# Cross-attention and a block-quantised feed-forward layer on one core: the first two steps in another order

## The reference

```
n   = layernorm(x)
k,v = split((ctx @ Wsrc.T + b_src) * mask)          # 8 heads of 16
q   = (n @ Wtgt.T + b_tgt) * mask
att = softmax(where(mask == 0, -inf, q k / 4)) v     # per sequence and head
x   = x + concat(n, att) @ Wout.T + b_out
g   = fp4(layernorm(x)) @ fp4(w_gate).T              # fp4: blocks of 16 along the last axis
u   = fp4(layernorm(x)) @ fp4(w_up).T
x   = x + fp4(silu(g) * u) @ fp4(w_down).T
```

## Time and profile before

| | |
|---|---|
| median of 3 runs | 218.21 us (218.11 to 219.34) |
| the profiled execution | 219.57 us |
| its span | 217.6 us |
| mean granted TensorE clock | 0.973 |
| loaded and stored | 11.97 MB |

### The profile page before, as it was taken

How to read it: one execution, slowest core, us unless ns; L and a number is a source line. 1 busy time by engine, 2 the same in 40 slices (tenths; PEclk the granted TensorE clock), 3 DMA queues, 4 the chain that set the end, 5 groups by cost and what they waited for, 6 DMA issues and landing times.

```text
span 217.6 us, 5689 instructions
## 1 busy us (share of the span) xinstructions
PE 187.8 (86%) x2045; PEld 141.5 (65%) x2045; DVE 176.5 (81%) x391; ACT 131.8 (61%) x264; POOL 139.3 (64%) x203
## 2 busy tenths in 40 slices
PE   0839988979998999998998998796898988899963
PEld 0318574856967769587696775475676766677753
DVE  6417785898799876978769987999999999999941
ACT  2362697957878877798786744364455383665441
POOL 6272737188969592672926577676689875777750
PEclk9985999999999999999999999699999999999998
DMA  6999632040200000000000000000101010101111
GB/s 190 268 293 345 225 115 81 7 144 3 96 3 5 3 0 0 5 3 3 0 3 5 0 5 0 0 0 2 50 3 48 0 48 3 48 2 51 48 49 48
DMA packets 13665, 11.97 MB, mean 55 GB/s; under 512 B 766, under 2 KB 10558, under 8 KB 13630
## 3 DMA queue, kind: packets, MB, share of 16 engines
q1 hardware_dynamic: 13078, 11.29, 16.8%
q10 hardware_dynamic: 560, 0.33, 0.5%
HBM read 9.52 MB, written 2.10 MB: 53 GB/s over the span
## 4 chain that ended last, share of the span: by engine, by line
PE 31%; POOL 20%; issue 14%; DVE 7%; ACT 4%; POOLq 0%; DVEq 0%; ACTq 0%
POOL hq L372 7%; POOL wq_y L357 5%; PE bank L890 4%; PE bank L946 4%; PE bank L949 3%; PE bank L899 3%; PE bank L900 2%; PE bank L878 2%; PE bank L970 2%; POOL xn L254 2%; ACT xn L411 2%; PE a_pair L841 2%; POOL sch L364 2%; PE bank L841 2%; ACT val L423 2%
## 5 line engine op out<-in xcount | busy, mean ns | idle before, releaser
L970 PE MATMUL bank<-wdT,hT 128*128 128x128 f32 x192 | 27.1, 278 | 4.1 <-issue 3.3
L946 PE MATMUL bank<-guT,xqT 128*128 128x352 f32 x64 | 25.5, 481 | 4.3 <-DVE hh L732 4.3
L372 POOL TENSOR_TENSOR hq<-wq_u,sch 128x704 f32<-128x704 f32 x16 | 22.6, 1410 | 9.5 <-DVE wq_u L759 9.4
L970 PEld LDWEIGHTS bank<-wdT,hT 128*128 128x128 f32 x192 | 23.9, 191 | 5.4 <-issue 4.4
L949 PE MATMUL bank<-guT,xqT 128*128 128x352 f32 x64 | 25.0, 473 | 0.0
L357 POOL TENSOR_TENSOR wq_y<-hh,ivh 128x704 f32<-128x704 f32 x16 | 22.5, 1407 | 3.9 <-DVE ivh L747 3.3
L878 PE MATMUL bank<-cT,wsT 128*128 128x512 f32 x32 | 16.9, 655 | 6.5 <-DMA cT<-in_ctxT 6.5
L477 ACT ACTIVATE mask_bc<-bank 128x352 f32<-128x352 f32 x32 | 14.7, 458 | 12.3 <-PE bank L946 12.3
L545 ACT COPY hT<-bank 128x384 f32<-128x384 f32 x32 | 15.2, 476 | 10.2 <-PE bank L958 10.2
L532 ACT ACTIVATE a_pair<-wq_y 128x704 f32<-128x704 f32 x16 | 12.2, 763 | 14.8 <-DVE wq_u L759 14.4
L612 DVE TENSOR_REDUCE den<-prob 128x8 f32<-128x512 f32 x32 | 19.8, 666 | 0.0
(11 more groups left out here) (117 smaller groups left out, 497.2 us busy)
## 6 DMA issues: line engine op xcount, KB each, us to landing
cT<-in_ctxT SPq DMA_DIRECT2D x8, 512.0 KB, 5.2
x_all<-in_x SPq DMA_DIRECT2D x8, 256.0 KB, 5.5
mask_bc<-in_mask_rows SPq DMA_DIRECT2D x8, 256.0 KB, 6.3
out_y<-mask_bc SPq DMA_DIRECT2D x8, 256.0 KB, 2.2
wsT<-in_WsT ACTq DMA_DIRECT2D x1, 256.0 KB, 4.2
w_all<-in_wg SPq DMA_DIRECT2D x1, 176.0 KB
w_all<-in_wu SPq DMA_DIRECT2D x1, 176.0 KB
w_all<-in_wd SPq DMA_DIRECT2D x1, 176.0 KB
```

Source lines behind the costliest of these rows:

```text
L372: nc.gpsimd.tensor_tensor(hq[i][:, :, 0:I].rearrange("p t (n k) -> p t n k", k=BLK), rh[i][:, :, :].rearrange("p (t n) k -> p t n k", t=2) ...
L946: nc.tensor.matmul(gu_bank[2 * n % 3][:, 0:I], xqT[g % 2][:, t], guT[:, 0, :], start=True, stop=True).then_inc(pe_g, 1)
L970: last = nc.tensor.matmul(d_bank[:, j * P:(j + 1) * P], hT[n % 2][:, c, :], wdT[:, c, :], start=(c == 0), stop=(c == 2))
```

## The change

The loads of the mask are cut in two: the columns of group 0 are loaded by themselves, two of four pieces on SP behind the first x and context, two on ScalarE's queue behind wsT; the rest follows on ScalarE's queue. The order on SP becomes x0, context 0, mask pieces, mask row 0, x1, context 1, the three weights, mask row 1, x2, and so on. POOL makes neg_mask of group 0 before the reciprocal deviation of group 0, and no bias nb for that group; VectorE normalises group 0 itself. On TensorE, 34 matmuls on constants run at the start; in step 0 only keys, transposes and queries of group 0 remain. Step 1 begins with the scores of group 0, then the values of group 0 and the keys of group 1; the bias of the values stands behind the values of group 1. VectorE's weight scales move from step 0 to step 1 ahead of the masked queries, the statistics of group 2 behind them, and the bias sum behind the reciprocals of the row sums. POOL's wq_y, the deviations of groups 2 and 3 and `add_bias(0)` move into step 1. From step 2 on ScalarE runs `normalise1` at the head of a step, ahead of `weight_evac` and `v_evac`.

```
# SP
             load_x(0)
             load_c(0)
+            sp.wait_ge(mb_zero, 1)
+            for p in range(PAIRS // 2):
+                load_pairs(sp, p, slice(0, TILES), ld_mb0)
+            load_m(0)
             load_x(1)
-            load_m(0)
-            sp.wait_ge(mb_zero, 1)
-            for p in range(PAIRS):
-                sp.dma_start(mask_b[32 * p:32 * p + 2, :, :]...).then_inc(ld_mb, 16)
+            load_c(1)
             sp.wait_ge(w_zero, 2)
             ...
-            load_c(1)
+            load_m(1)
             load_x(2)
...
# POOL
-            rstd1_of(0)
-            pool.wait_ge(ld_mb, 16 * PAIRS)
+            pool.wait_ge(ld_mb0, 16 * PAIRS)
             pool.wait_ge(mb_zero, 1)
             nc.gpsimd.tensor_scalar(neg_mask[:, tiles(0), :], ...).then_inc(nm_ok, 1)
+            rstd1_first()
             rstd1_of(1)
+            pool.wait_ge(ld_mb, 16 * PAIRS)
...
-            rstd1_of(2)
-            add_bias(0)
...
-                if on(g1) and g1 > 0:
-                    add_bias(g1)
-                if k == 0:
+                if k == 1:
                     pool.wait_ge(wiv_ok, 1)
                     nc.gpsimd.tensor_tensor(wq_y[:, :, :], ...).then_inc(wy_ok, 1)
+                    rstd1_of(2)
+                if on(g1) and g1 > 1:
+                    add_bias(g1)
...
                 if on(g2):
                     expand_reciprocals(g2)
-                if on(g1 + 3):
+                if k == 1:
+                    add_bias(0)
+                    add_bias(1)
+                    rstd1_of(3)
+                if on(g1 + 3) and k > 0:
                     rstd1_of(g1 + 3)
# ScalarE
             act.dma_start(wsT[:, :, :], ...).then_inc(ld_ws, 16)
+            act.wait_ge(mb_zero, 1)
+            for p in range(PAIRS // 2, PAIRS):
+                load_pairs(act, p, slice(0, TILES), ld_mb0)
...
-            normalise1(0)
+            act.wait_ge(mb_zero, 2)
+            for p in range(PAIRS):
+                load_pairs(act, p, slice(TILES, NT), ld_mb)
             def attn_step(k):
+                if on(g1) and k > 1:
+                    normalise1(g1)
                 if 0 <= k - 5 < 3:
                     weight_evac(k - 5)
                 if on(g2):
                     v_evac(g2)
...
-                if on(g1) and k > 1:
-                    normalise1(g1)
# VectorE
+            def normalise_first():
+                dve.wait_ge(rstd1, 1)
+                dve.wait_ge(aggr1, 1)
+                for j in range(TILES):
+                    last = nc.vector.tensor_scalar(xn[0][:, j, :], x_all[:, j, :], mv1[:, j, 0:1],
+                                                   rs1[:, j:j + 1], ALU.subtract, ALU.mult)
+                last.then_inc(xn_ok, 1)
...
+                if k == 1:
+                    weights_scales()
                 if on(g1):
                     q_masked(g1)
-                if k == 0:
-                    dve.wait_ge(bo_pe, 1)
-                    dve.wait_ge(ld_o, 32)
-                    (b_out sum)
-                    weights_scales()
+                if k == 1:
                     stats1(2)
                 (row sums, reciprocals)
                 if k == 1:
+                    (b_out sum, with its two waits)
                     stats1(3)
# TensorE
+            def warm_up():
+                for _ in range(34):
+                    nc.tensor.matmul(av_bank[:, 0:P], neg_ident[:, :], neg_ident[:, :], start=True, stop=True)
             pe.wait_ge(c_id, 3)
+            warm_up()
             def attn_step(k):
                 if on(g2):
                     scores(g2)
+                if k == 1:
+                    v_project(0, 0)
+                    v_project(0, 1)
+                    k_project(1)
...
                     q_project(0)
-                    bias_of_values()
                 elif on(g1):
                     xn_transpose(g1)
-                    k_project(g1)
+                    if k > 1:
+                        k_project(g1)
...
-                if on(g1):
+                if on(g1) and k > 0:
                     v_project(g1, 1)
+                if k == 1:
+                    bias_of_values()
```

More of the change, by code:

```diff
@@ L139, in xattn_ffn @@
         ld_m = [sem(f"ld_m{g}") for g in range(NG)]
-        ld_ws, ld_wt, ld_b, ld_o, ld_fw, ld_mb = (sem(n) for n in ("ld_ws", "ld_wt", "ld_b", "ld_o", "ld_fw", "ld_mb"))
+        ld_ws, ld_wt, ld_b, ld_o, ld_fw, ld_mb0, ld_mb = (
+            sem(n) for n in ("ld_ws", "ld_wt", "ld_b", "ld_o", "ld_fw", "ld_mb0", "ld_mb"))
         out_d = [sem(f"out_d{s}") for s in range(2)]
@@ L176, in past, with load_pairs @@
                 eng.wait_ge(semaphore, value)
+        def load_pairs(eng, p, t, loaded):
+            eng.dma_start(mask_b[32 * p:32 * p + 2, t, :].rearrange("b n s -> b (n s)"),
+                          mask_pairs[:, t.start * S:t.stop * S]).then_inc(loaded, 16)
         block = ctx.enter_context(nc.Block())
@@ L212, in _ @@
             sp.dma_start(b_out[:, 0, :], bo.to_broadcast([P, D])).then_inc(ld_o, 16)
-            load_m(1)
             load_x(3)
@@ L228, in _, with rstd1_first @@
         def _(pool):
+            def rstd1_first():
+                pool.wait_ge(aggr1, 1)
+                nc.gpsimd.tensor_scalar(ve1[:, tiles(0)], mv1[:, tiles(0), 1], EPS, 1.0, ALU.add, ALU.mult).then_inc(var1, 1)
+                pool.wait_ge(var1, 1)
+                nc.gpsimd.tensor_tensor(rs1[:, tiles(0)], ve1[:, tiles(0)], minus_half[:, :], ALU.pow).then_inc(rstd1, 1)
             def rstd1_of(g):
@@ L235, in rstd1_of @@
                 pool.wait_ge(rstd1, g + 1)
-                pool.wait_ge(nm1_ok, g + 1)
+                pool.wait_ge(nm1_ok, g)
                 nc.gpsimd.tensor_tensor(nb1[:, tiles(g)], nm1[:, tiles(g)], rs1[:, tiles(g)], ALU.mult).then_inc(nb1_ok, 1)
@@ L310, in _ @@
                                     ALU.mult, ALU.add).then_inc(nm_ok, 1)
+            rstd1_first()
             rstd1_of(1)
+            pool.wait_ge(ld_mb, 16 * PAIRS)
+            pool.wait_ge(mb_zero, 2)
             nc.gpsimd.tensor_scalar(neg_mask[:, TILES:, :], mask_b[:, TILES:, :], BIG, -BIG,
@@ L405, in normalise1 @@
             def normalise1(g):
-                act.wait_ge(nb1_ok, g + 1)
+                act.wait_ge(nb1_ok, g)
                 act.wait_ge(ld_x[g], 16)
@@ L567, in _ @@
         def _(dve):
-            nc.vector.memset(mask_b[:, :, :], 0.0).then_inc(mb_zero, 1)
+            nc.vector.memset(mask_b[:, 0:TILES, :], 0.0).then_inc(mb_zero, 1)
+            nc.vector.memset(mask_b[:, TILES:, :], 0.0).then_inc(mb_zero, 1)
             nc.vector.memset(w_all[64:P, 0:WBLK, :], 0.0).then_inc(w_zero, 1)
@@ L585, in stats1 @@
                 stats(g, st1, mv1, stat1, aggr1)
+            def normalise_first():
+                dve.wait_ge(rstd1, 1)
+                dve.wait_ge(aggr1, 1)
+                for j in range(TILES):
+                    last = nc.vector.tensor_scalar(xn[0][:, j, :], x_all[:, j, :], mv1[:, j, 0:1], rs1[:, j:j + 1],
+                                                   ALU.subtract, ALU.mult)
+                last.then_inc(xn_ok, 1)
             def stats2(g):
@@ L681, in _ @@
             nc.vector.tensor_scalar(bk_of[:, :], head_of[:, :], b_k, None, ALU.mult).then_inc(c_bk, 1)
+            normalise_first()
             stats1(1)
@@ L712, in attn_step @@
                 if k == 1:
+                    dve.wait_ge(bo_pe, 1)
+                    dve.wait_ge(ld_o, 32)
+                    nc.vector.tensor_tensor(b_out[:, 0, :], o_bank[:, 0:D], b_out[:, 0, :], ALU.add).then_inc(bo_ok, 1)
                     stats1(3)
```

2 lines of the change are left out of this document (removed).

## The result

The changed kernel takes 213.59 us (median of 4 runs, 212.46 to 216.25), the kernel before 218.5 us on the same chip. The ratio is 0.9743, with a 95% interval of 0.9689 to 0.9797: 2.6% faster. The forecast was 211.2, in a range of 208.8 to 214.8.

What follows compares the result with a forecast made beforehand. The prediction took the start as bound by order of work on TensorE, not a resource. 5.4 us head start at step 2 plus 1.6 in steps 5 to 7 gives 7.0; 218.2 - 7.0 = 211.2, range 208.8 to 214.8.

Steps and rivals of the forecast that it cites:

- main case: Whole kernel: the forecast with its unknown costs of mask rows, VectorE's normalise and step 1; 210 to 213 us, chance 0.57.
- the clock falling before 14: TensorE at the start: a granted clock falling before 14 us would show the prediction wrong.
- Mask rows at 6.6: Start: split mask pieces of group 0 land between 6.5 and 7.3 us, taken as 6.6, instead of 11.24.
- Rival (a): Start: mask rows land late, at 11.24; first scores slip 4.6 us, gain 2.4, time 215.8; chance 0.11.
- xn ready at 9.2: Group 0: normalised x ready at 9.2 us after neg_mask, variance, power and VectorE's normalise, against 10.0 before.
- First scores at 12.4: TensorE, group 0: scores start at 12.4 us after transposes, copy, queries and masked queries, instead of 19.78; 7.4 us earlier.
- Step 1 takes 12.8 us: Group 0 scores to group 1 scores: 10.84 becomes 12.8 us; scores -0.75, values 2.1, uncovered copy 0.4, bias 0.25.
- Rival (c): Steps 1 and 2: x or context of group 2 or 3 lands late, giving 214.2 to 216.6 us; chance 0.10.
- (d): VectorE in step 1 waits at the weight scales for late weights, making the kernel slower; chance 0.03.
- Rival (e): TensorE's 1.59 us stop in `attend(1)` moves where it waits anyway; gain 8.6, time 209.6; chance 0.12.
- Steps 5 to 7, 1.6 us: ScalarE's normalise ahead of value copies removes TensorE's 0.53 us stop before the transposes, three times: 1.6 us.
- rival (b): Start: warm-up fails to raise the clock or gaps let it fall; about 5 us more, time 216; chance 0.07.

Runs made afterwards that it cites:

- first profile: Traced execution of the changed kernel, compared with the kernel before: 216.25 us, span 214.5, the granted clock falling in the queries of group 0.
- second profile: Trace from timing the changed kernel again, nothing altered, beside the kernel before: span 211.3; that run's median 213.31 us, ratio 0.9737.
- the two edits filled: Kernel before with the bias sum moved and ScalarE's normalise first, plus 76 matmuls of 128 columns in TensorE's step 0 gaps: 215.39 us, ratio 0.9833.

## Why the prediction was right

The sign and the range were right; the median came out 2.4 us above the forecast. It lies above the 210 to 213 of the main case too, in the part of the range that was kept for late mask rows and late loads, and neither of these happened; what came in their place was a shorter head start, the base below and, in the longest execution, the clock. The ratio, taken on the 218.21 us that the prediction started from, gives 212.6, inside the main case. So the range is right either way, but the median is in it partly by luck. One of the signs of being wrong, the clock falling before 14, was there in the first profile (0.62 at 12.5 to 13.4), and with it a slow value block. By the steps of the prediction, against the second profile of the changed kernel, in which the clock holds:

- **Mask rows at 6.6.** Right, 6.51 (6.24 in the first profile). Rival (a) is out.
- **VectorE's normalise, 0.8.** 1.11, near the upper bound of 1.16.
- **xn ready at 9.2.** Wrong, 10.3. The step that failed is what is queued behind what: I listed the work behind `rstd1_first` on VectorE, but not `bk_of`, ahead of the normalise there. Its load now goes behind the mask pieces on ScalarE's queue and lands at 9.1 to 9.3 instead of by 6.4 (in the profile without the warm-up it landed at 6.65, so the order alone doesn't fix it). The run with the key biases behind the normalise puts this at 0.9 us. Why the load lands by 6.65 in one execution and at 9.1 or later in two others stays open.
- **x of group 1 at 8.3.** Wrong, 11.0, but hidden: its statistics end 0.6 us before the queries.
- **First scores at 12.4.** 13.73: 1.1 of it from xn, the rest from the steps between.
- **Step 1 takes 12.8 us.** Right, 12.88. The head start at group 1 is 4.0 instead of 5.4.
- **Nothing in steps 2 to 4.** Right, 28.0 before and after from group 2 to 4. Rival (c), loads late, is out, and so is (d): no wait for the weights. Rival (e) is out as well: the stop of 1.59 us is gone from this profile and nothing was gained by it.
- **Steps 5 to 7, 1.6 us.** Mechanism right, size 2.2 (1.9 in the first profile, 2.3 alone).
- **The base.** The sum of 7.0 was made in the profiled execution of 219.57 us and taken off the median of 218.21. That execution lay 1.4 us above the median, with more of the low clock in it (0.973 in the mean) than most, so part of what I took off was not in the median. Between the profiles the gain is 6.3 us (217.6 to 211.3), between the medians 4.9 to 5.7.
- **The clock, rival (b) with 0.07.** Its mechanism is real, and I weighed it too low. The prediction said that no gap of the length of 2.61 us is left; the late key biases leave one of 2.0 to 2.4 ahead of the transposes, and the clock fell behind the longer one. It costs about 2.6 us there, not 5. It does not explain the median: the second profile, at full clock throughout, took 213.06 us, already 0.8 above the lowest run of 212.3 and 0.25 below the median. Of those 0.8 us the wait for the key biases can be most; no second execution was traced to show it.

What the prediction did not see at all is which parts carry the gain. The order on ScalarE gives 1.9 to 2.3 us in every profile that has it (steps 5 to 7 take 38.2 to 38.6 instead of 40.5). The bias sum out of step 0 gives 4.6 against the profile before when the clock holds: 1.5 are the place of the bias matmul, 0.7 an output bias that landed late in that profile, and 2.4 work that it did at the low clock. These two alone reach a span of 210.5, against 210.5 to 211.3 for the changed kernel at full clock. In such executions, as far as the profiles show, the split mask loads, the warm-up, VectorE's normalise and the scores ahead of the values add nothing: the values, 2 us, are only moved into step 1. Against the two edits alone the whole change has the lower median (213.3 against 215.0), but they were timed on different chips and the intervals of their ratios touch (0.9703 to 0.9771, 0.9747 to 0.9846), so it is not shown that it is more often in the better case. If it is, neither the warm-up nor its 34 matmuls are the reason, since the kernel without them has the ratio 0.9747.

## What to carry to other kernels

Find the first place where an engine is idle although its next useful operation has all its inputs, and move only what stands in between; here two changes of order gave, in their best executions, what a rewrite of the first two steps gave. A filler of a few wide matmuls in the idle gaps of the start made the two edits steady (a spread of 0.06 instead of 3.3 us) at their lowest time, a ratio of 0.974 where they had 0.9796 without it; that equals the changed kernel's 0.974 with far fewer edits. Whether it works by the clock or by where TensorE's stops fall is not separated: its trace has both full clock throughout step 0 and no stop. The same filler in 76 narrow matmuls gave 0.9833, with a stop in the wrong place. Before an edit that lets an engine wait for one load more, list everything ahead of the operation in its queue, small loads too, and make the sum against an execution whose clock is that of the median.

## What was unexpected of the hardware

- **TensorE can stop inside a group of short matmuls that wait for nothing**: 1.0 to 1.6 us in `attend(1)` in the six kernels with 2045 matmuls, 1.8 to 2.75 in `attend(0)` with 76 matmuls more. It happens where 64 matmuls are issued in 1.1 us, and always behind the same matmul by count, the 470th or the 346th.
- **A gap can be paid twice.** After 2.35 and 2.75 us without work the granted clock read 0.51 and 0.50, and the four key matmuls of a group took 2.34 and 3.50 us instead of 1.88. After the 1.82 us of the two edits filled it read 1.00.
- **The clock column and the durations can disagree.** In the profile of ScalarE's order alone the granted clock reads 1.00 throughout, and the values of group 0 take what they take in the earlier trace rows at 0.50:

```profile
16.39 3.62 PE L890 MATMUL bank<-wsT,cT 128*128 128x128 f32 x16
```

- **A load of 1.5 KB took between 4.4 and 7.1 us to land in the same order of loads**, with two pieces of 2 KB ahead of it and the bulk loads beside it: 7.1 in the first profile of the changed kernel, 6.8 in the second, 5.4 with the key biases behind the normalise and 4.4 without the warm-up (from issue to landing). In the kernel before it took 4.9.
